# Expert layer: the down products of two steps issued together, and the ring sizes that go with it

## What is computed

```python
x = x + rwkv(layernorm(x))
x = x + ffn(layernorm(x))        # moe1: the change is in its routed part
x = x + retention(layernorm(x))
x = x + ffn(layernorm(x))        # moe2

def ffn(x):                      # 4096 tokens, E = 64 experts, F = 64, D = 256, 4 choices per token
    scores = softmax(x @ router_w)
    top = top_k(x @ router_w + router_bias, 4)
    comb[token, top] = normalised scores
    g = silu(einsum('nd,edf->nef', x, wg))
    u = einsum('nd,edf->nef', x, wu)
    routed = einsum('ne,nef,efd->nd', comb, g * u, wd)
    shared = sum over 2 shared experts of (silu(x @ swg) * (x @ swu)) @ swd
    return routed + shared
```

## Time and profile before

| | |
|---|---|
| median of 3 runs | 1624.3 us (1621.7 to 1625.3) |
| the profiled execution's own time | 1625.95 us |
| its span, first to last instruction | 1624.2 us |
| PE busy in the span | 1322.5 us, 81% |
| DVE, ACT, POOL busy | 69%, 42%, 57% |
| routed part of moe1 | 408.3 us to 617.2 us after the span's start |

### The profile page before, as it was taken

The page is one execution under the profiler, slowest core; times in us unless marked ns, Lnnn a source line. Parts: engine busy times, 40 slices in busy tenths (PEclk is TensorE's granted clock), DMA queues, the critical chain, the costliest instruction groups (busy, mean ns, idle before and its releaser), DMA issues. The chain is left out here.

```text
span 1624.2 us, 25154 instructions
## 1 busy us (share of the span) xinstructions
PE 1322.5 (81%) x7400; PEld 882.2 (54%) x7400; DVE 1115.7 (69%) x2766; ACT 680.2 (42%) x1365; POOL 930.7 (57%) x1064
## 2 busy tenths in 40 slices
PE   6688467996999997799887888855999588888664
PEld 2344344664777773456464565642666466666433
DVE  4899887775466563418475573768677488888768
ACT  5999321221566663141404224221121376677520
POOL 3999547776455555264544543017777377777700
PEclk9799768998899997999988889967999799999978
DMA  9900073334777764224335142044232666664178
GB/s 362 388 1 0 5 298 104 107 108 144 238 248 248 252 224 152 63 79 170 138 112 190 41 158 107 2 174 177 103 113 98 201 201 194 208 195 155 29 282 275
DMA packets 116745, 257.61 MB, mean 159 GB/s; under 512 B 22759, under 2 KB 44686, under 8 KB 116116
## 3 DMA queue, kind: packets, MB, share of 16 engines
q1 hardware_dynamic: 88436, 188.51, 33.9%
q0 software_dynamic: 27648, 67.70, 12.3%
q10 hardware_dynamic: 544, 0.00, 0.0%
HBM read 124.76 MB, written 139.75 MB: 163 GB/s over the span
## 5 line engine op out<-in xcount | busy, mean ns | idle before, releaser
L853 POOL DMA_INDIRECT slots_x<-arena,slot x256 | 271.7, 1061 | 104.6 <-issue 74.2
L1185 POOL DMA_INDIRECT pairs_y<-arena x192 | 189.4, 987 | 79.0 <-issue 44.9
L1109 PE MATMUL moe_narrow<-arena 128*128 128x128 f32 x1536 | 209.3, 280 | 30.5 <-DVE arena L1250 29.9
L1109 PEld LDWEIGHTS moe_narrow<-arena 128*128 128x128 f32 x1536 | 188.7, 193 | 42.4 <-issue 42.1
L698 PE MATMUL moe_wide<-arena 128*128 128x512 f32 x384 | 186.7, 633 | 17.9 <-DVE arena L966 17.9
L1250 DVE TENSOR_TENSOR arena<-arena,moe_narrow 64x128 f32<-64x128 f32 x384 | 111.6, 291 | 107.1 <-ACT arena L1152 101.3
L457 POOL DMA_INDIRECT arena<-slots_y,slot x128 | 125.9, 984 | 93.2 <-DMA arena<-slots_y,slot 49.2
L1146 ACT ACTIVATE arena<-moe_narrow 128x512 f32<-128x512 f32 x192 | 114.7, 597 | 108.9 <-PE moe_narrow L1109 55.3
L1098 PE MATMUL moe_narrow<-ident,arena 128*128 128x128 f32 x768 | 128.3, 291 | 21.2 <-DMA arena<-slots_x 21.2
L485 DVE SCALAR_TENSOR_TENSOR residual<-arena,gate,residual 128x256 f32<-128x256 f32 (+1 forms) x256 | 113.0, 514 | 39.4 <-DMA arena<-pairs_y 19.0
L1258 DVE COPY arena<-moe_wide 128x512 f32<-128x512 f32 x192 | 132.8, 692 | 8.8 <-DMA pairs_y<-arena 2.7
(11 more groups left out here) (253 smaller groups left out, 2423.8 us busy)
## 6 DMA issues: line engine op xcount, KB each, us to landing
slots_x<-arena SPq DMA_DIRECT2D x48, 528.0 KB, 4.9
arena<-slots_x SPq DMA_DIRECT2D x96, 264.0 KB, 3.0
slots_x<-arena SPq DMA_DIRECT2D x48, 512.0 KB, 15.2
arena<-slots_x SPq DMA_DIRECT2D x96, 256.0 KB, 3.1
slots_y<-arena SPq DMA_DIRECT2D x96, 256.0 KB, 2.3
arena<-w_gu SPq DMA_DIRECT2D x2, 8192.0 KB
arena<-pairs_y SPq DMA_DIRECT2D x32, 512.0 KB, 4.6
residual<-x SPq DMA_DIRECT2D x8, 512.0 KB, 8.7
```

What stands on the lines that cost most here:

```text
L853: pool.indirect_dma_start(out=x_slots, in_=xn[:, t, :], in_offset=None, out_offset=bass.IndirectOffsetOnAxis(ap=slot[:, t, i:i + 1], axis=0))\
L1109: last = pe.matmul(h_ps[n % 2][:, j * P:(j + 1) * P], weights[:, n % 3, j, h, :], xt[:, n % XTRING, (j * KH + h) * P:(j * KH + h + 1) * P] ...
L1185: pool.indirect_dma_start(out=slots.y_of, in_=ytile[:, n % YRING, j, :], in_offset=None, bounds_check=slots.pairs - 1, oob_is_err=False, o ...
```

## The change

Only moe1 is changed. TensorE does `down` for two pairs one after the other in every odd step, where it did one in every step. VectorE's list has in an odd step first `multiply` and then `keep_y`, and in an even one `keep_y` and then `multiply`, as before. The rings `ht` and `wd_pair` have four places, and `xin` has five where it had six.

```diff
-    XRING, XTRING, YRING, RING = (8, 2, 4, 8) if scatters else (6, 3, 4, 8)
+    XRING, XTRING, YRING, RING = (8, 2, 4, 8) if scatters else (5, 3, 4, 8)
+    HTRING = 3 if scatters else 4
...
-    ht = arena.take(3, 2 * P)
-    wd_pair = arena.take(3, D)
+    ht = arena.take(HTRING, 2 * P)
+    wd_pair = arena.take(HTRING, D)
...
             for s in range(NP + DOWN):
...
                 if HIDDEN <= s < NP + HIDDEN:
                     hidden(s - HIDDEN)
-                if s >= DOWN:
+                if scatters:
+                    if s >= DOWN:
+                        down(s - DOWN)
+                elif s > DOWN and (s - DOWN) % 2:
+                    down(s - DOWN - 1)
                     down(s - DOWN)
...
             def stage_down(n):
...
-                if n >= 3:
-                    act.wait_ge(exp_sem("y_full"), n - 2)
+                if n >= HTRING:
+                    act.wait_ge(exp_sem("y_full"), n - HTRING + 1)
...
             def multiply(n):
                 dve.wait_ge(exp_sem("sig_ready"), n + 1)
-                if n >= 3:
-                    dve.wait_ge(exp_sem("y_full"), n - 2)
+                if n >= HTRING:
+                    dve.wait_ge(exp_sem("y_full"), n - HTRING + 1)
...
             for s in range(HIDDEN, NP + DOWN + 1):
+                together = not scatters and (s - DOWN) % 2
+                if together and s < NP + HIDDEN:
+                    multiply(s - HIDDEN)
                 if s > DOWN:
                     keep_y(s - DOWN - 1)
...
-                if s < NP + HIDDEN:
+                if not together and s < NP + HIDDEN:
                     multiply(s - HIDDEN)
```

More of the change, by code:

```diff
@@ L1121, in down @@
                     rows = slice(j * F, (j + 1) * F)
-                    last = pe.matmul(y_ps[n % 2][:, j, 0:D], ht[rows, n % 3, j * P:(j + 1) * P],
-                                     wd_pair[rows, n % 3, :], start=True, stop=True)
+                    last = pe.matmul(y_ps[n % 2][:, j, 0:D], ht[rows, n % HTRING, j * P:(j + 1) * P],
+                                     wd_pair[rows, n % HTRING, :], start=True, stop=True)
                 last.then_inc(exp_sem("y_full"), 1)
@@ L1158, in stage_down @@
                     load_experts(mybir.EngineType.Activation, held, n)
-                if n >= 3:
-                    act.wait_ge(exp_sem("y_full"), n - 2)
+                if n >= HTRING:
+                    act.wait_ge(exp_sem("y_full"), n - HTRING + 1)
                 for j in range(0 if scatters else 1, 2):
-                    act.activation(wd_pair[j * F:(j + 1) * F, n % 3, :], down_of(held[n][j]), ACT.Copy)\
+                    act.activation(wd_pair[j * F:(j + 1) * F, n % HTRING, :], down_of(held[n][j]), ACT.Copy)\
                         .then_inc(exp_sem(f"wd_ready{j}"), 1)
@@ L1206, in stage_down @@
                     pool.wait_ge(k.wd_in, 16 * WD_LOADS * turn)
-                if n >= 3:
-                    pool.wait_ge(exp_sem("y_full"), n - 2)
-                pool.tensor_copy(wd_pair[0:F, n % 3, :], down_of(held[n][0])).then_inc(exp_sem("wd_ready0"), 1)
+                if n >= HTRING:
+                    pool.wait_ge(exp_sem("y_full"), n - HTRING + 1)
+                pool.tensor_copy(wd_pair[0:F, n % HTRING, :], down_of(held[n][0])).then_inc(exp_sem("wd_ready0"), 1)
             for s in range(NP + HIDDEN):
@@ L1245, in multiply @@
                 dve.wait_ge(exp_sem("sig_ready"), n + 1)
-                if n >= 3:
-                    dve.wait_ge(exp_sem("y_full"), n - 2)
+                if n >= HTRING:
+                    dve.wait_ge(exp_sem("y_full"), n - HTRING + 1)
                 for j in range(2):
                     cols = slice(j * P, (j + 1) * P)
-                    product = dve.tensor_tensor(ht[j * F:(j + 1) * F, n % 3, cols], sig[F:2 * F, n % 2, cols],
+                    product = dve.tensor_tensor(ht[j * F:(j + 1) * F, n % HTRING, cols], sig[F:2 * F, n % 2, cols],
                                                 h_ps[n % 2][F:2 * F, cols], ALU.mult)
```

## The result

The changed kernel took 1611.07 us (median of 4 runs, 1604.76 to 1611.9) beside 1624.53 us before: a ratio of 0.9912, 95% interval 0.9891 to 0.9933. A second series of five runs gave 1611.46 against 1623.65, ratio 0.9924 (0.9910 to 0.9937). So the medians gained 12 to 14 us where 16.3 had been forecast. The profiled execution took 1610.83 us of its own, 15.1 less than the one before.

The account below looks back on a forecast made before the run. TensorE was taken to bound moe1's routed part. Joining saves 16.9 us, the end gives back 0.6: 16.3 less than the profiled 1625.95 is 1609.7, or 1608.0 against the 1624.3 median; range 1602.5 to 1613.5, chance 83%.

Parts of the forecast that it names:

- What bounds the part: Routed part of moe1: TensorE sets the pace, 2.113 us a step, with no matmul waiting for another engine.
- the price of a join: moe1 down products: an isolated group costs 0.78 us, a second directly behind it 0.43, so joining two saves 0.35.
- The rival of exposed loads: Joined down products: the second pair's weight loads aren't hidden, second down costs 0.65 us, kernel 1618.2 us; chance 3%.
- The end: Last pairs of moe1: from the last joined group's start to the last copy's end about 4.0 us, 0.6 longer.
- The sum of the part: Routed part of moe1: 16.9 us saved up to the last group, 0.6 given back at the end, 16.3 less.
- the schedule: Offsets in the new 3.87 us cycle of moe1: the odd multiply ends 1.7 us before the hidden products needing it.
- the y buffers: Down products' buffers in moe1: 1.4 us of slack, 0.5 us of cover when ACT's row comes 1.2 late, the thinnest.
- the rival of small waits: moe1: transfers hold TensorE, with other small waits such as ACT's late rows; 4.7 us lost, 1612.7 us; chance 8%.
- Sum: 16.9 - 0.6 = 16.3 us less: moe1's saving up to the last copy, subtracted from the whole kernel's profiled 1625.95 us to give 1609.7.
- no change: moe1 steps stay at 2.113 us, as something unnamed sets the pace or transfers keep their rate: 1624 us; chance 3%.
- slower: moe1: emptying both y buffers in one go delays the second product, losing 0.46 us against 0.35 gained: 1630.0; chance 3%.

Follow-up runs that it names:

- full_rows_single: Kernel before, but each moe1 down product takes all 128 array rows (result not the layer's), single groups: 1633.64 us in one run, step 2.196 us.
- rings_only: Kernel before with only the new ring sizes (ht and down weights four, x five), old TensorE and VectorE order: ratio 1.0025 to the kernel before.
- pairs_old_rings: Changed kernel but with the old rings, three for ht and down weights and six for x: ratio 0.9912 to the kernel before.
- pairs_old_dve: Changed kernel but with VectorE copying first and multiplying then in every step: ratio 0.9921 to the kernel before.
- pairs_only_tensor: Kernel before with only TensorE's down calls joined in twos, old rings and VectorE order: 1608.17 us, ratio 0.9914 to the kernel before.
- full_rows_pairs: Changed kernel, but each moe1 down product takes all 128 array rows (result not the layer's): 1632.60 us in one run, cycle 4.389 us.
- both_layers: Kernel before with TensorE's down calls joined in twos in moe1 and also in moe2: ratio 0.9868 to the kernel before.

## Why the prediction was right

**What bounds the part, and the price of a join.** Both held. The steps went from 2.113 to 3.87 / 2 us, the joined group costs 0.43 more than a lone one, hidden products are followed by transposes without a gap. full_rows_single shows the cause that the prediction could only read from two gaps: a change of array rows. rings_only, pairs_old_rings, pairs_old_dve and pairs_only_tensor show that TensorE's order alone makes the gain.

**The rival of exposed loads** fell: 8 matmuls in 1.13 to 1.14 us, in group after group, where exposed loads would have made it 1.35. The rule of the Trainium skill (TensorE: Matmul & The Clock Gate, Part 3, Packing small matmuls), that loads overlap only when the row groups differ, does not hold here.

**The end.** From the start of the last joined group ahead of `down(94)` to the end of the last copy I had 4.0 us. It is 595.71 to 599.71 in the timeline:

```profile
595.71 1.13 PE L1123 MATMUL moe_wide<-arena 64*128 64x256 f32 x8
597.68 1.30 PE L1123 MATMUL moe_wide<-arena 64*128 64x256 f32 x8 [0.84 <-DVE arena L1263]
...
598.42 1.29 DVE L1263 COPY arena<-moe_wide 128x512 f32<-128x512 f32 x2 [0.29 <-PE moe_wide L1123]
```

**The sum of the part** came out at 17.1 us less (208.2 to 191.1) for 16.3, and that it is so near is in part luck: two terms that I did not have nearly cancel. The first is the start: transposes of the seventh pair came 12.44 us after the first ones before, 10.21 now. One join is 0.35 of these 2.23 us. The rest is not the change's: in the second profile of the changed kernel it was 10.64, at a clock of 0.50 from 410 to 413 us and not the 0.73 of the first; TensorE's order alone with the ring of six took 10.65; full_rows_single, with nothing joined and the ring of six, took 10.14. The profile of the kernel before had a slow start, and my sum was compared with it. From the seventh transposes on my terms give 16.3 - 0.35 = 15.9 us, and the traces 14.9 and 14.2 us less, with 1.2 and 1.9 us of small waits in them. Without the waits that is 16.1 both times, so the price of a join is right within a few tenths in 46.

The second term is these small waits: 1.2 us in seven cycles in the first profile, 1.9 us in seven in the second. The largest of the first is 0.52 us. In ACT's timeline, where registers are loaded:

```profile
458.47 0.38 ACT L1157 ACTIVATE arena<-moe_narrow 64x256 f32<-64x256 f32 x1 [0.30 <-PE moe_narrow L1110]
460.82 0.42 ACT L1167 ACTIVATE arena<-arena 64x256 f32 x1 [1.98 <-PE moe_wide L1123]
...
462.16 0.40 ACT L1167 ACTIVATE arena<-arena 64x256 f32 x1
```

ACT's row came 2.07 us late (460.82 - 458.47 less the usual 0.28). I had taken 1.2 from one row, and in the kernel before it was 1.14 to 1.20 at all 11 places with a register load from 428 us on. In the changed kernel four of the 11 stayed there, six came 1.56 to 1.67 us late and this one 2.07. Why the same load became longer is not shown; the down product that this row also waits for, and that the profile names, had ended more than 3 us earlier. VectorE's multiply then came at 462.29 after an idle time of 2.82, and the hidden products that need it started at 463.00, 0.12 us after its end. In the schedule they had 1.7 us of cover, less than the 2.07; the y buffers, whose cover I had called the thinnest, held. In six of the seven longer cycles it is this wait for the multiply (1.0 us in all), in the seventh one for x.

Among the waits of the changed kernel between 425 and 595 us these are the rows of TensorE:

```profile
PEld moe_narrow L1099 <- issue: 13.9, 42, 0.3
...
PEld moe_narrow L1099 <- DMA arena<-slots_x: 0.6, 1, 0.6
PEld moe_narrow L1110 <- POOL arena L1057: 0.5, 1, 0.5
...
PE moe_narrow L1110 <- DVE arena L1255: 0.3, 1, 0.3
PE moe_narrow L1099 <- DMA arena<-slots_x: 0.2, 1, 0.2
```

The wait that is put down to POOL L1057 is the same one at 463.00: the weights needed there had been ready for 3.65 us, and the copy of that moment stands where it does in an undisturbed cycle. So the rival of small waits, for transfers and for ACT's late rows, was there beside the forecast, at a quarter of its 4.7 us in the first profile and two fifths in the second. Loads of x landed after 3.6 us in the median for 3.0, at most 5.5.

**The step that was too large** is "Sum: 16.9 - 0.6 = 16.3 us less", taken as the whole kernel's. It ended at the last copy and assumed that all that follows only moves. It does not quite. From the end of the last copy to the first gather of the sum part passed 619.57 - 617.15 = 2.42 us before and 603.53 - 599.71 = 3.82 now; the last store landed 2.0 us after the last copy before and 3.4 now. Of the 17.1 us 1.4 are given back there. The second profile of the same kernel gave back 2.0 (4.42 for 2.42) and was only 13.6 us ahead of the one before at that first gather (605.94 for 619.57). The other runs speak for the joining as the cause: the same stretch is 2.42 in full_rows_single and 4.13 in full_rows_pairs, and 3.2 to 4.6 in all runs with joined products. They don't prove it, since rings_only, with nothing joined, has 3.63 on its chip. My sum of 16.3 less the small waits and this hand-over is 13.7 and 12.4 us, and the medians gained 13.5 and 12.2. From there to the end the parts move about as well: 16.0 us ahead at the gather became 15.1 at the end of the span in the first profile, 13.6 became 13.2 in the second, 16.0 became 17.7 in that of pairs_only_tensor.

**The cases of no change and of slower** did not come up. The time lies inside the range, 2.4 us under its upper end.

## What to carry to other kernels

Look for gaps on TensorE where matmuls on half the array's rows stand between matmuls on all of them, and put the half-row ones of several steps next to each other: each join here saved 0.35 us, with no other edit needed. Before joining more, write down what stands ahead of each product that TensorE will need next; joining four put VectorE's copies ahead of a multiply that the hidden products wait for, and over a third of what two had gained was lost. Cost the hand-over behind the part as well: here 1.4 to 2.0 us of 17 went there. And when a wait row names an engine, look up when that engine's result was ready: in two of these kernels rows named GpSimd, whose weights had long been there. Last, compare starts among several traces before a difference of 2 us there is put down to the change.

## What the runs showed of the hardware

The kernel before took 1624 us on some chips, and 1859.36 (median of 35 runs) and 1832.83 us (11 runs) on the two that ran rings_only and both_layers. The routed part of moe1 was as fast there, with steps of 2.113 us and cycles of 3.87. The time went elsewhere: in rings_only the first transposes of moe1 came at 477.0 us, and at 408.3 in the profile of the kernel before on its own chip, and from the first to the last transposes moe2 took 331.2 us instead of 237.7. In the routing part ahead of moe1 its waits have gaps of up to 16.2 us put down to issue. What slows those chips was not looked into; the ratios agree with those of the fast chips.
